# Gated cross attention and routed experts on one core: the gate folded into the output projection, the heads' sums gathered and spread by transfers

## The reference

```
x = x + tanh(g_xattn) * attention(layernorm(x), ctx, ctx, adj, mask)
x = x + tanh(g_ffn)   * experts(layernorm(x))

attention: Q = heads(layernorm(x)), K, V = heads(ctx)         16 heads of 16 columns
  scores = Q K^T / 4 + adj, -inf where mask == 0;  weights = softmax(scores)
  out = (weights V, heads side by side) Wo^T + bo
experts:   gate_probs = softmax(h gate_w^T);  e = argmax;  w = gate_probs[e]
  out = w * (relu(h w1[e] + b1[e]) w2[e] + b2[e])
```

## Time and profile before

| | |
|---|---|
| time, median of 3 runs | 554.51 us (552.46 to 555.67) |
| span of the profiled execution, first to last instruction | 548.5 us |
| median less span (start and end outside the instructions) | 6.0 us |
| start-up, until the first mask | 0 to 28.0 |
| batches 0 to 3, first mask to first mask | 28.0, 113.9, 199.7, 284.6, to about 370 |
| last tail with the early experts | 370 to 414 |
| loop of 18 expert tiles | 414 to 548.5 |

### The profile page before, as it was taken

One profiled execution on the slowest core, in us unless ns is written; L12 is line 12 of the kernel. 1 busy time (PEld: TensorE's weight loads), 2 busy tenths in 40 slices (PEclk: granted clock), 3 DMA queues, 4 the chain that ended last, 5 costly groups with the idle time before them and its releaser, 6 DMA issues. The chain is left out here.

```text
span 548.5 us, 13306 instructions
## 1 busy us (share of the span) xinstructions
PE 526.3 (96%) x4123; PEld 405.1 (74%) x4124; DVE 302.3 (55%) x923; ACT 309.1 (56%) x678; POOL 297.9 (54%) x424
## 2 busy tenths in 40 slices
PE   8999999989999999999999999888999999999997
PEld 5577667667666667666676666658899999999996
DVE  2776587976677887668885878845340211111111
ACT  4366678665678665778675676664332333333322
POOL 5346566665567575468574556555244444443451
PEclk9999999999999999999999999999999999999999
DMA  8633625400405510204520057499136665555570
GB/s 288 206 110 132 192 65 183 149 31 6 150 21 192 166 50 1 79 10 153 180 85 1 11 184 250 147 362 320 59 103 218 211 205 196 178 187 184 189 210 1
DMA packets 51489, 77.67 MB, mean 142 GB/s; under 512 B 9945, under 2 KB 34601, under 8 KB 51305
## 3 DMA queue, kind: packets, MB, share of 16 engines
q1 hardware_dynamic: 46600, 67.72, 37.0%
q0 software_dynamic: 4192, 8.73, 5.0%
q10 hardware_dynamic: 640, 0.52, 0.3%
HBM read 52.76 MB, written 8.35 MB: 111 GB/s over the span
## 5 line engine op out<-in xcount | busy, mean ns | idle before, releaser
L1588 DVE CUSTOM_DVE_ANT_0 prob<-bank,adjm 128x512 f32<-128x512 f32 x256 | 172.3, 688 | 70.6 <-issue 39.9
L1229 ACT ACTIVATE pt<-bank 128x512 f32<-128x512 f32 x256 | 152.1, 596 | 87.7 <-PE bank L951 81.2
L682 POOL TENSOR_SCALAR prob<-prob,negmax 128x512 f32<-128x512 f32 x190 | 132.0, 698 | 117.6 <-DVE negmax L1588 113.4
L951 PE MATMUL bank<-ident,prob 128*128 128x128 f32 x1024 | 154.8, 274 | 2.2 <-POOL prob L682 1.3
L951 PEld LDWEIGHTS bank<-ident,prob 128*128 128x128 f32 x1024 | 124.2, 141 | 39.7 <-issue 13.7
L1299 ACT ACTIVATE adjm<-bank,colsm 128x128 f32<-128x128 f32 x184 | 52.6, 368 | 105.0 <-PE bank L1127 80.0
L940 PE MATMUL bank<-w2s 128*128 128x512 bf16 x256 | 97.5, 381 | 8.5 <-DVE negmax L1588 5.7
L963 PE MATMUL bank<-pt,vals 128*32 128x256 f32 x1024 | 68.3, 385 | 0.9 <-DVE vals L1386 0.5
L1127 PEld LDWEIGHTS bank<-xT,pt 128*128 128x128 f32 x576 | 67.1, 192 | 0.9
L1127 PE MATMUL bank<-xT,pt 128*128 128x128 f32 x576 | 67.2, 275 | 0.0
L1137 PE MATMUL bank<-w2s,adjm 128*128 x288 | 65.1, 379 | 0.0
(11 more groups left out here) (195 smaller groups left out, 624.4 us busy)
## 6 DMA issues: line engine op xcount, KB each, us to landing
pt<-in_L_ffn_w SPq DMA_DIRECT2D x19, 1024.0 KB
w2s<-parts SPq DMA_DIRECT2D x96, 128.0 KB
w2s<-in_L_ffn_w SPq DMA_DIRECT2D x8, 1024.0 KB
maski<-in_mask_Bx1xSxS_ik SPq DMA_DIRECT2D x4, 1024.0 KB, 5.6
w2s<-parts SPq DMA_DIRECT2D x56, 64.0 KB, 2.1
xres<-in_x SPq DMA_DIRECT2D x18, 128.0 KB
x_d<-rows SPq DMA_DIRECT2D x18, 128.0 KB
xn_d<-rows SPq DMA_DIRECT2D x18, 128.0 KB
```

The lines of the kernel that those rows point to most:

```text
L682: po.tensor_scalar(prob[:, m], prob[:, m], -1.0, negmax[:, m:m + 1], ALU.mult, ALU.add).then_inc(s_shpool, 1)
L951: mm = pe.transpose(tr_bank[n % NTB][:, c * P:(c + 1) * P], prob[:, n % TILES % NB, c * P:(c + 1) * P], ident[:])
L1229: act.activation(pt[:, g % 2, :, j, q2 * P:(q2 + 1) * P], tr_bank[c % NTB][:].rearrange("p (c q) -> p c q", c=QT), ACT.Exp).then_inc(s_cac ...
L1588: ve.tensor_tensor_reduce(out=prob[:, m % NB], in0=sc_bank[m % NS][:], in1=adjm[:, qt], scale=-1.0, scalar=BIG, op0=ALU.add, op1=ALU.min, ...
```

## The change

**Gate folded.** The gate's rows are centred (their mean taken off, `centre` on DVE), so that the gate can be applied ahead of the normalization: the logits are rstd times (new x times the centred gate). New x is the old x plus tanh(g) times the projection, so `woT` becomes 264 columns wide: 256 of `Wo` and 8 of `Wo` times gate ("fold", once, in PE's step 9). What the old x gives is computed from its transposed, normalized form (`xT`) by a new use "gate x", times its standard deviation `std`. "out" then yields the logits as 8 more columns of `rows`, and POOL multiplies them by rstd. "normed" and "gate" are gone.

**Heads' sums by transfers.** For the four batches "heads" and "turn" are gone (the last two tiles of the last batch keep them). SP copies the heads' columns from `o_sb` closely packed to `oc` (`compact`, four transfers for half the heads) and the 16 sums to `rc`, 16 partitions x 256; DVE takes the reciprocal of `rc` (`invert`); SP spreads it over the partitions (`spread`, four transfers); DVE multiplies 128 x 512 into `atT` (`scale`).

**Order.** SP's issues, and the steps of the uses and of the tables, are set anew.

```diff
-    TAIL_A = [(15, "heads", 0), (18, "heads", 1), (23, "turn", 0), (25, "turn", 1), (29, "out", 0),
-              (33, "out", 1), (38, "normed", 0), (41, "normed", 1), (44, "gate", (0, 1)), (51, "rank", 0)]
+    TAIL_A = [(29, "out", 0), (33, "out", 1), (51, "rank", 0)]
...
+    SUMS_STEPS, SCALE_STEPS = ((15, 47), (13, 45)), ((20, 53), (18, 50))
...
+            def compact(par, qh):
+
+                for j in range(HG):
+                    to = slice(par * P // 2 + j * D, par * P // 2 + (j + 1) * D)
+                    sp.dma_start(oc[to], o_sb[j * VW:j * VW + D, par::2, qh]).then_inc(t_comp, 16)
+                if par == 1:
+                    sp.dma_start(rc, o_sb[D:P:VW, :, qh]).then_inc(t_sums, 16)
+
+            def spread(b, half):
+
+                sp.wait_ge(t_rc, b * 2 + half)
+                for a in range(NG):
+                    at = a % 2 * P // 2
+                    sp.dma_start(rs[at:at + P // 2, a // 2], rc[a:H:NG].rearrange("j (o q) -> j o q", o=1).to_broadcast(
+                        [HG, D, HALF])).then_inc(t_over, 16)
...
-                for u in range(2):
-                    rows_out(b, (t + (NT - 2)) % NT, u)
-                    sp.wait_ge(s_parts, (b + 1) * 4 + 3)
-                    stack_in(sp, par, 0, u, 0, EC, range(PAIRS), s_stack)
+                compact_new(b, 0)
+                rows_out(b, (t + (NT - 2)) % NT, 0)
+                sp.wait_ge(s_parts, (b + 1) * 4 + 3)
+                stack_in(sp, par, 0, 0, 0, EC, range(PAIRS), s_stack)
+                rows_out(b, (t + (NT - 2)) % NT, 1)
+                compact_new(b, 1)
+                stack_in(sp, par, 0, 1, 0, EC, range(PAIRS), s_stack)
+                spread(b, 1)
                 rows_free(b, 0)
-                sp.wait_ge(s_parts, (b + 1) * 4 + 4)
                 for g in range(NQ):
                     stack_in(sp, par, 1, g, 0, EC, range(PAIRS), s_stack)
...
+                po.wait_ge(t_rstd, b * 4 + k + 1)
+                po.tensor_scalar(logit[:, (k + 2) % 4], rows[:, u, E:EX], rstd2[:, u:u + 1], None, ALU.mult
+                                 ).then_inc(t_logit, 1)
...
-                if what == "gate":
-                    pe.wait_ge(t_x2T, b * 4 + k[-1] + 1)
+                if what == "gate x":
                     o = bank_free(b, i)
-                    for j, kk in enumerate(k):
-                        for c in range(EC):
-                            mm = pe.matmul(o[:, j * X:(j + 1) * X], x2T[:, kk % 2, c], gateT[:, c],
+                    for c in range(EC):
+                        for t in range(QT):
+                            mm = pe.matmul(o[VW * t:VW * (t + 1), 0:P], gateT[:, c], xT[:, c, t * P:(t + 1) * P],
                                            start=c == 0, stop=c == EC - 1)
...
+            def invert(b, half):
+
+                ve.wait_ge(t_sums, 16 * (b * 2 + half))
+                ve.reciprocal(rc, rc).then_inc(t_rc, 1)
+
+            def scale(b, half):
+
+                ve.wait_ge(t_comp, COMPACT * (b * 2 + half))
+                ve.wait_ge(t_over, SPREAD * (b * 2 + half))
+                ve.tensor_tensor(atT[:], oc[:], rs[:], ALU.mult).then_inc(t_atT, 1)
```

More of the change, by code:

```diff
@@ L340, in build @@
         FIRST = 16 * 2 * PAIRS
+        COMPACT = 16 * 2 * HG
+        SPREAD = 16 * NG
         STACKED = NQ * FIRST
@@ L474, in _ @@
             last = B - 1
-            tail_pair(last, last * QT - 2, 0, last * QT)
+            compact_old(last, 1)
+            spread(last, 0)
             sp.wait_ge(s_score, last * TILES)
@@ L920, in tail_use @@
                 if what == "out":
-                    pe.wait_ge(t_atT, b * 4 + k + 1)
+                    pe.wait_ge(t_atT, b * 2 + (k // 2 + 1 if b < B else k + 1))
                     o = bank_free(b, i)
+                    if k == 0 and b < B:
+                        pe.wait_ge(s_xgs, b + 1)
+                        pe.transpose(o[:, EX:EX + P], xgs[:], ident[:])
                     for c in range(EC):
-                        mm = pe.matmul(o[:, 0:E], atT[:, u, c], wT[:, 3, c], start=c == 0, stop=c == EC - 1)
-                if what == "normed":
-                    pe.wait_ge(t_row, b * 4 + k + 1)
-                    o = bank_free(b, i)
-                    for c in range(EC):
-                        mm = pe.transpose(o[:, c * P:(c + 1) * P], rows[:, u, E + c * P:E + (c + 1) * P],
-                                          ident[:])
+                        mm = pe.matmul(o[:, 0:EX], atT[:, c, u * P:(u + 1) * P], woT[:, c], start=c == 0, stop=c == EC - 1)
                 mm.then_inc(s_m, 1)
@@ L989, in step @@
                 for i, what, k in at_step(uses, n):
-                    if what == "heads" and k == 2:
-                        pe.wait_ge(s_osb, b * GROUPS + (NG + 2))
                     if what == "values":
@@ L1017, in _ @@
                 if n == GATE_STEP:
-                    pe.wait_ge(s_gatew, 16)
+                    pe.wait_ge(s_gc, 3)
                     o = bank_free(0, setup_at("gate"))
                     for k in range(EC):
-                        mm = pe.transpose(o[:, k * X:(k + 1) * X], gate_r[:, k * P:(k + 1) * P], ident[0:X, 0:X])
+                        mm = pe.transpose(o[:, k * VW:(k + 1) * VW], gate_r[:, k * P:(k + 1) * P], ident[0:VW, 0:VW])
                     mm.then_inc(s_m, 1)
+                if n == FOLD_STEP:
+                    gate = setup_at("gate")
+                    pe.wait_ge(s_md[gate % 2], free(0, gate) + 1)
+                    for c in range(EC):
+                        for m in range(EC):
+                            pe.matmul(pv_bank[:, c * X:(c + 1) * X], wraw[:, 3, m, c * P:(c + 1) * P], gateT[:, m, 0:X],
+                                      start=m == 0, stop=m == EC - 1)
+                    pe.wait_ge(s_gc, 6)
+                    pe.matmul(pv_bank[:, EC * X:(EC + 1) * X], xgs[0:VW], ident[0:VW, 0:X], start=True, stop=True
+                              ).then_inc(s_wog, 1)
             for b in range(B - 1):
@@ L1600, in step @@
                         row_stats(b, k)
+                if n in SUMS_STEPS[last] and (b > 0 or n != SUMS_STEPS[0][0]):
+                    invert(b, SUMS_STEPS[last].index(n))
+                if n in SCALE_STEPS[last] and (b > 0 or n != SCALE_STEPS[0][0]):
+                    scale(b, SCALE_STEPS[last].index(n))
                 if n in ROW_STEPS[last]:
@@ L1615, in step @@
                     if n == FIRST_RANK[0]:
-                        route_shift(b, [i for i, (k, w, a) in enumerate(LAST_USES) if w == "gate" and a in ((2,), (3,))],
-                                    B, *RANKED[0])
+                        route_shift(B, B * 4, *RANKED[0])
                     if n == FIRST_RANK[1]:
```

251 lines of the change are left out of this document (158 added, 93 removed).

## The result

The changed kernel is slower, by 0.8%. Its median is 556.84 us (11 runs, 555.25 to 559.94) against 552.77 us (11 runs, 550.26 to 555.67) of the kernel before, run beside it on the same chip: ratio 1.0079, interval 1.0057 to 1.0101. The prediction of 542.5 us, and its range to 551.0, are wrong. The profiled execution has a span of 555.3 us, before 548.5 us. One run of the last experiment's kernel, 734 us at a granted clock of 0.655, is left out of its ratio.

The account below looks back on a forecast made before the run. The prediction took PE as the bound, with DVE nearly as late in places of steps 40 to 55. Savings 9.6 + 2.1 + 1.0 - 1.0 = 11.7 us took the median from 554.5 to 542.5 us, range 537.0 to 551.0.

Parts of the forecast that it names:

- the one on SP: Thirteen added transfers a batch on SP's queue: sums and spread waits put at nothing, stacks fit with 1.4 us to spare.
- Rival 1: Transfers of sums and spread land at 5.8 us, not 2.1; 9.8 us of the gain go: 552 us, chance 0.09.
- What PE is spared: Transposes and gate matmuls removed, less added work: net 4.03 us a batch; 3.2 counted in batches 0 to 2, 9.6 in all.
- friction: Steps 40 to 55, where DVE is nearly as late as PE: 0.8 us a batch of PE's saving not counted.
- What DVE gets: DVE's work per batch: +2.2 us net, with reciprocals at 1.93 us each; steps 40 to 55 need 18.6 us.
- Batch 3: Last batch, steps 40 to 55 held by DVE's index tables: saves 2.1 us instead of 4.03.
- The last tail: After the last batch, "normed" and "gate" leave the chain: net 1.0 us saved.
- Start-up: The fold on PE and `centre` on DVE before the batches: costs 1.0 us once, bounds 0 to 2.5.
- Rival 3: The last 16 stacks miss the start of the batch, making the kernel slower: 558 us, chance 0.07.
- Rival 2: DVE is the bound: each reciprocal stops PE for another 0.8 us, 5.6 us go: 548 us, chance 0.14.

Follow-up runs that it names:

- the last experiment's kernel: Changed kernel with eight stacks issued by ScalarE and the out of k = 2 and 3 later, sums and spread still late: ratio 1.0012 to the kernel before.

## Why the prediction was wrong

**The step that failed is the one on SP**, "I put these waits at nothing". Its arrival times were right. Counted from the start of batch 2 (199.7 before, 204.5 after), I had `compact` begin at 257.5 - 199.7 = 57.8 and end at 59.6 to 61.0 us, and the last of the sums land by 63.1 (at 2.1 us) or 64.3 (at 3.3). They began at 261.49 - 204.5 = 57.0, ended at 61.0, and DVE started on the sums at 62.4. What I had wrong is when they are wanted. I took 263.6 from the trace of before, 63.9 us into its batch; the changed kernel was there at 264.50 - 204.5 = 60.0. It is the change that brings it forward: PE, spared the transposes and the gate's matmuls, brings DVE to the end of mask 47 some 4 us sooner, while SP's queue, which from 251.4 on waits for nothing but its own issues, came to `compact` only 0.8 us sooner (57.0 against 57.8). I set the need of the stacks earlier by what I expected to save, and did not do so for the sums. The arrival at 62.4 less 60.0 is the 2.36 us of the trace; in batches 0 and 1 the same wait was 2.26 and 1.66 us, where the sum had nothing. For the spread the error is the same: it stood behind eight stacks until 270.69, with the reciprocal done at 268.6.

**Rival 1** (transfers come late, 552, chance 0.09) was the right mechanism for the wrong reason: nothing had to land slowly. Its price was near: two waits a half at 0.7 us, 9.8 us in all, where the runs put both orders together at 1.55%, 8.5 us. The trace has nine such waits, 13.3 us on DVE. That its 552 us is still short of the 556.8 measured comes from the gain of 11.7 us that it was subtracted from, which was too high.

**What PE is spared** was spared: no lines for `normed` and `gate`, PE busy 9.9 us less, `gate x` at 0.65 us a batch, not 0.85. But I priced it as time wherever PE was the fullest engine. With the transfers in time the first three batches gain 0.1, 1.5 and 1.9 us (85.9, 85.8 and 84.9 us before), not 3.2 each. With eight stacks on ACT and the out of k = 2 and 3 later too, they gain 2.9, 3.0 and 1.2, with part of the stacks' wait still there. The term was mis-sized less by its count than by two limits behind it, the late stacks and DVE's pile in steps 56 to 63, of which the prediction had friction of 0.8 us in steps 40 to 55 only. DVE's pile, which the move of both out steps made, has no line in it, and the stacks were given 1.4 us to spare. So this is a second step that failed: even with the sums and the spread in time the kernel gains 0.76%, 4.2 us, and not 11.7.

**What DVE gets.** The reciprocal took 1.735 us, not 1.93, and not the estimate of 2.13 worked out from the Trainium skill (VectorE: DVE Perf Modes, First, the fixed hardware budget); `scale` 0.69 as taken. DVE's busy time in steps 40 to 55 was 8.90 + 8.21 = 17.1 us, I had 17.4. They lasted 21.9 and not 18.6: the fill was 78%, for DVE stood.

**Batch 3** gave nothing instead of 2.1 us: 77.3 us from its first mask to its last, against 77.2. Steps 40 to 47 took 11.9 us with DVE at 10.45, and turning the issues changed nothing there. With the fold alone it was 75.9, so the fold is worth 1.3 us there and the heads' part (78.0 alone) loses it. That it loses it on DVE is shown in part: with the two reciprocals of this batch replaced by copies it is 75.0 and not 76.4 with both transfers early, and 76.1 and not 77.3 with the changed kernel's order. **The last tail** did not give its 1.0 us. PE finished `weigh` 9.8 us behind the last mask, not 7.8, and from there to the end of the span it is 179.3 us against 178.9. Why `weigh` ended later was not separated by a run (7.3 to 10.4 us in the other traces). **Start-up** cost 0.5 us at the first mask (28.4 against 27.9); what the fold cost in steps 6 to 9 isn't told apart from `gate x`.

**Rival 3** (the last 16 stacks come late) did not happen in the changed kernel, and happened as soon as it was made faster (7.4 us of waits of PE in three batches): it caps what a gain ahead of it can bring. **Rival 2** (DVE is the bound) holds in part: its reciprocals cost about 3 us, and the pile of steps 56 to 63 is worth something once fewer stacks are late.

## What to carry to other kernels

When a change makes one engine faster, every arrival has to be set against the need in the new time scale: what hangs on a serial queue does not move forward with it. In such a queue, put first the transfer on which something else depends in turn (here the sums, then their spread), and what is wanted a batch later behind it; the order of nine issues was enough here to turn the sign of the whole change. And a step that removes one of two waits that lie beside each other can show nothing, or a loss: try them together before either is called free, and then look whether the other has come back.

## What was not expected of the hardware

**What an issue costs SP does not go with its size.** In issues that follow one another it was 0.60 us for the sums' 16 KB, 0.64 for a stack's 128 KB (5.08 us for eight), 0.60 for a spread's 64 KB, and 0.65 to 0.85 for the gathers' 32 KB. Finished rows of 128 KB took 0.32 to 0.59, and a mask's 1 MB 0.38. The price of many small transfers is here the issuing.

**The clock falls behind a stall, and adds to what it costs.** After the wait in step 47 PE's granted clock is at 0.50, the 1.2 GHz level, for some 3 us (from:to, length, PE, PEld, DVE, ACT, POOL, clock):

```profile
267.00:269.00 2.00, 0.79 (x6) 0.42 (x4) 1.93 (x4) 1.94 (x5) 0.00 (x0) 1.00 0.63 209
269.00:271.00 2.00, 0.94 (x4) 0.79 (x5) 1.72 (x7) 0.03 (x1) 0.69 (x1) 0.69 0.60 202
271.00:273.00 2.00, 2.00 (x20) 1.69 (x19) 2.00 (x7) 1.32 (x2) 0.72 (x2) 0.50 0.42 138
273.00:274.00 1.00, 1.00 (x10) 0.64 (x12) 0.93 (x6) 0.72 (x2) 1.00 (x2) 0.92 0.28 95
```

PE had been busy 0.79 of 2 us, and then nothing up to 270.06. Four transposes took 1.06 us there instead of 0.60. In the heads-only kernel the reciprocal of step 47 waited 0.96, 2.82 and 1.15 us in the three batches, and the clock fell after the first two only. Steps 48 to 55 of batches 1 and 2:

```profile
181.40:191.60 10.20, 8.75 (x75) 6.17 (x78) 8.68 (x29) 4.32 (x7) 5.45 (x8) 0.83 0.52 171
...
269.00:277.80 8.80, 7.46 (x75) 5.23 (x78) 8.29 (x29) 4.42 (x8) 4.19 (x7) 1.00 0.45 146
```

The fall goes with 1.4 us more. That it causes all of that was not tried by itself.

How much of the loss can this be? In the changed kernel the granted clock is at 0.50 five times ahead of the end (three of them behind the waits of step 47, one at the turn to batch 1, one in the last tail), in the kernel with both transfers early three times, in the kernel before never. An estimate from these traces: some 3 us at half of the clock cost at most half of that, 1.5 to 2 us. So up to 3 or 4 us of the 8.5 can be the clock's, and not the waits' alone; no run separates the two.

**The last tail differs from one group of runs to another.** From the last mask to the end it is 186.7 and 189.0 us in the first traces (before, after), 183.8 to 186.6 in the eight traces of the first two groups of experiments, and 189.1 to 189.6 in the four of the last two. In the long ones, the two first traces among them, ACT waits up to 3.3 us at a time for something that the profile calls remote, and PE 1.9 to 2.0 us for DVE's `region`, whatever the kernel. Counted from the end of `weigh`, it is 178.9 to 179.5 us in the six long ones and 175.9 to 177.5 in the eight short ones. The cause stays open.
